# Scaled maxima of two attentions evicted by ScalarE and added by GpSimd, smaller VectorE chains, one context buffer, in a four-layer cross-attention stack

## What is computed

```python
# L0 (attentions 0 and 1): queries, keys and values without bias, 16 heads of 16
energy = einsum('bhsk,bhtk->bhst', Q, K)
lengths = sum(energy[:, :, 0, :] != 0, axis=-1)          # per head, from row 0
energy = where(cols >= lengths, -inf, energy)            # causal mask too in attention 0
z = softmax(energy / sqrt(dk)) @ V * mask                # mask: tokens with any feature != 0
x = layernorm(x + z)                                     # then relu feed-forward behind attention 1
# L1 (2 and 3): biases, output weights, masks given; gelu feed-forward (1024) behind attention 3
# L2 (4): 16 heads of 64, no mask.   L3 (5): 16 heads of 16, biases
```

## Time and profile before

| | |
|---|---|
| median of 3 runs | 2408.44 us (2404.12 to 2409.41) |
| the profiled execution | 2405.55 us, its span 2403.8 us |
| busy: TensorE, VectorE, ScalarE, GpSimd | 2345.7, 1541.7, 1368.9, 856.5 us |
| first TensorE instruction | at 4.04 us, after ScalarE's copies of the identity |
| first products of K and Q | 8.30 to 12.08 us |
| first scores | at 17.49 us |
| slot of attention 0 in the first round | 8.60 us from scores step to scores step |

### The profile page before, as it was taken

How to read it: one execution, slowest core, us unless ns; L and a number is a source line. 1 busy time by engine, 2 the same in 40 slices (tenths; PEclk the granted TensorE clock), 3 DMA queues, 4 the chain that set the end, 5 groups by cost and what they waited for, 6 DMA issues and landing times.

```text
span 2403.8 us, 73575 instructions
## 1 busy us (share of the span) xinstructions
PE 2345.7 (98%) x30353; PEld 1975.7 (82%) x30353; DVE 1541.7 (64%) x3410; ACT 1368.9 (57%) x3238; POOL 856.5 (36%) x1444
## 2 busy tenths in 40 slices
PE   8999999999989999999998999999999899999998
PEld 6788888888778888888877888888887788888887
DVE  6886654446888664444688866444478886644446
ACT  4556655546556666554655666654465566655455
POOL 2464322223346432222334743222333463312232
PEclk9999999999999999999999999999999999999999
DMA  5300000000100000000010000000001000000000
GB/s 157 133 3 2 3 2 1 1 1 11 44 5 2 3 2 2 1 1 1 17 40 2 2 3 2 1 1 1 1 24 33 2 2 3 2 2 1 1 1 19
DMA packets 23789, 32.48 MB, mean 14 GB/s; under 512 B 2304, under 2 KB 22176, under 8 KB 23328
## 3 DMA queue, kind: packets, MB, share of 16 engines
q1 hardware_dynamic: 23456, 27.78, 3.6%
HBM read 23.57 MB, written 4.19 MB: 12 GB/s over the span
## 4 chain that ended last, share of the span: by engine, by line
PE 90%; POOL 3%; DVE 3%; issue 3%; ACT 1%; DMA 0%; SPq 0%; POOLq 0%; DVEq 0%; ACTq 0%
PE M L580 51%; PE SC L776 14%; PE M L586 10%; PE M L810 6%; PE SC L792 3%; PE M L827 3%; PE SC L624 2%; POOL Kx L1344 1%; DVE nmax L1223 1%; POOL seen_diag L1361 1%; POOL Y L1370 1%; POOL rstd L1376 0%; ACT Pr L973 0%; POOL q L1331 0%; ACT Qx L952 0%
## 5 line engine op out<-in xcount | busy, mean ns | idle before, releaser
L580 PE MATMUL M<-XT,W 128*128 128x128 f32 x4096 | 523.3, 277 | 0.0
L580 PEld LDWEIGHTS M<-XT,W 128*128 128x128 f32 x4096 | 490.6, 192 | 13.7 <-issue 3.3
L1223 DVE TENSOR_REDUCE nmax<-SC 128x8 f32<-128x1024 f32 x320 | 390.5, 1220 | 121.0 <-PE SC L776 120.2
L1344 POOL TENSOR_SCALAR Kx<-K,own,k_ones 128x128 f32<-128x128 f32 x640 | 289.0, 466 | 313.5 <-PE SC L776 225.6
L776 PE MATMUL SC<-Kx,Qx 32*128 32x128 f32 x5120 | 365.6, 280 | 14.9 <-DVE Kx L1202 8.8
L776 PEld LDWEIGHTS SC<-Kx,Qx 32*128 32x128 f32 x5120 | 317.4, 186 | 71.4 <-issue 59.9
L982 ACT ACTIVATE Pr<-SC 128x1024 f32<-128x1024 f32 x256 | 263.2, 1028 | 191.2 <-PE SC L776 191.2
L776 PE MATMUL SC<-Qx,Kx 32*128 32x128 f32 x5120 | 371.6, 283 | 0.1
L1376 POOL TENSOR_TENSOR rstd<-rstd,half 128x1 f32<-128x1 f32 x256 | 171.7, 671 | 502.4 <-DVE rstd L1297 500.5
L776 PEld LDWEIGHTS SC<-Qx,Kx 32*128 32x128 f32 x5120 | 310.4, 186 | 2.9 <-issue 2.4
L952 ACT ACTIVATE Qx<-M,q_bias,q_scale 128x128 f32<-128x128 f32 x640 | 241.1, 460 | 122.5 <-PE M L580 120.9
(11 more groups left out here) (144 smaller groups left out, 4091.4 us busy)
## 6 DMA issues: line engine op xcount, KB each, us to landing
X<-x SPq DMA_DIRECT2D x32, 128.0 KB, 2.2
c_in<-ctx_in SPq DMA_DIRECT2D x32, 128.0 KB, 2.2
out<-X SPq DMA_DIRECT2D x32, 128.0 KB, 1.7
RV<-row_vec SPq DMA_DIRECT2D x1, 2304.0 KB, 8.7
W<-w_k SPq DMA_DIRECT2D x5, 256.0 KB, 4.0
W<-w_q SPq DMA_DIRECT2D x5, 256.0 KB, 4.1
W<-w_v SPq DMA_DIRECT2D x5, 256.0 KB, 3.9
W<-w_f SPq DMA_DIRECT2D x1, 1024.0 KB, 6.4
```

Source lines behind the costliest of these rows:

```text
L580: last = pe.matmul(dst, a, b, start=(k == 0), stop=(k == len(lhsTs) - 1))
L1223: dve.tensor_reduce(nm, SC[h][:, :].rearrange("p (g c t) -> p g c t", c=KC, t=P), AX_X, ALU.max, negate=True).then_inc(maxima, 1)
L1344: last = pool.tensor_scalar(kx[:, half_of, c * P:(c + 1) * P], k[:, c * P:(c + 1) * P], own[:, half_of:half_of + 1], k_ones[:, half_of, c: ...
```

## The change

Nine things change.

1. In attentions 0 and 1, ScalarE evicts the transposed maxima with the scale `spare` into a new `max_row` (one buffer), and GpSimd adds both halves to `Qx` in one instruction (*max rows*). The step ST waits for that addition (`rows_added`).
2. The length chain: the count comes out of the comparison (`accum_out`), so the reduction goes; `steps` holds whole numbers and the factor is in `spare_big`.
3. The comparisons with 0 of seen tokens go from VectorE to GpSimd.
4. The addition of eps goes from VectorE to GpSimd (*rstd* now two instructions); `mv` has two buffers.
5. One context buffer: the load of sequence b waits until TensorE has turned b-1.
6. VectorE's setup: memsets first, masks last, and a semaphore `scales_done` ahead of the masks, for which ScalarE's Q and GpSimd wait.
7. TensorE makes the mask tables as its fourth step, behind the first K and Q.
8. SyncE doesn't wait for the setup, except for the mask rows.
9. The tables NARROW, OWN and BROAD have new numbers for nearly all items.

```diff
-NARROW = dict(XT=-1.22, SM=-1.27, K=-0.92, Q=-0.86, L=-0.4, V=0.3, CT=0.32, MT=0.86, PV=2.66, E1=3.2, E2=3.56,
+NARROW = dict(XT=-1.2, TM=-2.02, SM=-1.29, K=-0.92, Q=-0.86, L=-0.38, V=0.3, CT=0.15, MT=0.86, PV=2.62, E1=3.2,
...
-OWN = {0: dict(max=0.09, rXT=-0.07, V=0.44, q0=-0.67, residual=3.23, exp=0.06, rE1=0.09, keys=-1.37, rPV=0.23, K=-1.19,
-               rV=-0.04, MT=1.42, rK=-0.04, rMT=-0.16, rQ=-0.03, XT=-1.45, L=-0.44, PV=2.82, seen0=-1.26, Q=-0.58,
+OWN = {0: dict(max=0.11, rXT=0.04, V=0.46, q0=-0.8, residual=2.76, exp=0.07, rE1=0.11, keys=-1.31, rPV=-0.12, K=-1.1,
+               rV=0.04, MT=1.05, rK=0.09, rMT=0, rQ=-0.01, XT=-1.55, L=-0.4, PV=2.98, seen0=-0.63, Q=-0.58, CT=0.69,
+               LN=3.34, LNe=0.53, rL=0.01, seen1=4.35, E1=3.16, rCT=0.09, rMP=-0.29),
...
+MAX_BY_POOL = (0, 1)
...
-            put("POOL", n + o["SM"] - 0.20, "token mask", n)
+            put("POOL", n + o["TM"], "token mask", n)
...
-        tile(n + o["MT"], "DVE", o["rMT"], "MT", n)
+        if a in MAX_BY_POOL:
+            tile(n + o["MT"], "ACT", o["rMT"], "MT", n)
+            put("POOL", n + o["MT"] + o["rMP"], "max rows", n)
+        else:
+            tile(n + o["MT"], "DVE", o["rMT"], "MT", n)
...
-        put("SP", slot(b, 0) - 2.0, "context", b)
+        put("SP", slot(b, 0) - 0.75, "context", b)
...
-                    if b >= 2:
-                        sp.wait_ge(tile_full, done("tile", ("CT", b - 2)))
+                    if b >= 1:
+                        sp.wait_ge(tile_full, done("tile", ("CT", b - 1)))
...
-                if step == 1:
+                if step == 3:
                     make_tables()
...
-                        evicted(("MT", t_u // 2))
+                        if att(t_u // 2) in MAX_BY_POOL:
+                            pe.wait_ge(rows_added, done("max_rows", t_u // 2))
+                        else:
+                            evicted(("MT", t_u // 2))
...
+                elif kind == "MT":
+                    n = it[1]
+                    i = AT["max_rows"][n]
+                    if i >= 1:
+                        act.wait_ge(rows_added, i)
+                    for half_of in range(2):
+                        last = act.activation(max_row[0][:, half_of, :], tile_of(it)[:, 0:P], ACT.Copy,
+                                              scale=spare[:, half_of:half_of + 1])
+                    last.then_inc(tile_act, 1)
...
-                    dve.tensor_scalar(ne[:, :], tile_of(it)[:, 0:P], spare_row[:, 0:1], -1.0 / BIG, ALU.not_equal,
-                                      ALU.mult).then_inc(tile_dve, 1)
+                    dve.tensor_scalar(ne[:, :], tile_of(it)[:, 0:P], spare_row[:, 0:1], 0.0, ALU.not_equal,
+                                      ALU.add, accum_out=cnt[:, :]).then_inc(tile_dve, 1)
                     dve.wait_ge(tile_dve, done("tile_dve", it))
-                    dve.tensor_reduce(cnt[:, :], ne[:, :], AX_X, ALU.add).then_inc(len_cnt, 1)
-                    dve.wait_ge(len_cnt, done("length", n))
...
+                elif kind == "max rows":
+                    n = it[1]
+                    pool.wait_ge(tile_act, done("tile_act", ("MT", n)))
+                    q = on_ring(Qx, "narrow", n)[:, :, :].rearrange("p h (c t) -> p h c t", t=P)
+                    pool.tensor_tensor(q, q, on_ring(max_row, "max_rows", n)[:, :, :].unsqueeze(2)
+                                       .to_broadcast([P, 2, KC, P]), ALU.add).then_inc(rows_added, 1)
...
                 elif kind == "rstd":
                     key = it[1:]
+                    pool.wait_ge(var_done, done("norm", key))
...
+                    pool.tensor_scalar(r[:, :], on_ring(mv, "norm", key)[:, 1:2], EPS, None,
+                                       ALU.add).then_inc(eps_done, 1)
                     pool.wait_ge(eps_done, done("norm", key))
```

More of the change, by code:

```diff
@@ L230, in make_orders @@
             put("DVE", n + o["seen1"], "seen1", b)
+            put("POOL", n + o["seen1"] + 0.02, "seen1", b)
         if a in XT_FOR_FF:
@@ L304 @@
     "q0": [it[1] for it in pick("POOL", {"q0"})],
+    "max_rows": [it[1] for it in pick("POOL", {"max rows"})],
     "e1": [it[1] for it in pick("DVE", {"E1"})],
@@ L420, in build @@
         x_loaded, stored = [sem(f"x_loaded{i}") for i in range(LANES)], [sem(f"stored{i}") for i in range(LANES)]
-        c_loaded, m_loaded = [sem(f"c_loaded{i}") for i in range(2)], sem("m_loaded")
-        ready_act, ready_dve = sem("ready_act"), sem("ready_dve")
+        c_loaded, m_loaded = sem("c_loaded"), sem("m_loaded")
+        ready_act, ready_dve, scales_done = sem("ready_act"), sem("ready_dve"), sem("scales_done")
         setup = sem("setup")
@@ L690, in _ @@
                     b = it[1]
[L691 to L692 removed]
+                    pe.wait_ge(c_loaded, 16 * (b + 1))
+                    turn(tile_of(it), c_in[0], KC).then_inc(tile_full, 1)
                 elif kind == "BT":
@@ L1028, in then @@
                 dve.wait_ge(setup, n)
+            dve.memset(half[:, :], -0.5)
+            dve.memset(ones_b[:, :], 1.0)
+            for i in range(3):
+                dve.memset(V16[i][:, :, DK:DK + 1], 1.0)
+                dve.memset(V16[i][:, :, DK + 1:32], 0.0)
+            dve.memset(mask_i[:, :], 0)
+            for i in range(2):
+                dve.memset(nmax[i][:, :], 0.0)
+                dve.memset(q0[i][:, :, :], 0.0)
             dve.wait_ge(consts_in, 16)
@@ L1068, in _ @@
             at = CB_AT["q4"]
-            dve.tensor_scalar(CB[:, at:at + 8], CB[:, at:at + 8], DK2 ** -0.5, None, ALU.mult)
-            for i in range(3):
-                dve.memset(V16[i][:, :, DK:DK + 1], 1.0)
-                dve.memset(V16[i][:, :, DK + 1:32], 0.0)
-            dve.memset(mask_i[:, :], 0)
-            for i in range(2):
-                dve.memset(nmax[i][:, :], 0.0)
-                dve.memset(q0[i][:, :, :], 0.0)
+            dve.tensor_scalar(CB[:, at:at + 8], CB[:, at:at + 8], DK2 ** -0.5, None, ALU.mult).then_inc(scales_done, 1)
+            dve.wait_ge(all_masks_in, 16)
+            dve.tensor_scalar(Pr[2][0:BATCH, P:2 * P], Pr[2][0:BATCH, 0:P].bitcast(I32), 0.0, -BIG, ALU.is_equal,
+                              ALU.mult).then_inc(bias_done, 1)
+            dve.wait_ge(masks_in, 16)
+            dve.tensor_scalar(whole(0), Pr[1][:, 0:P].bitcast(I32), 0.0, -BIG, ALU.is_equal,
+                              ALU.mult).then_inc(mask_whole, 1)
             dve.wait_ge(masks_turned, 1)
@@ L1373, in _ @@
                     key = it[1:]
+                    pool.wait_ge(var_done, done("norm", key))
+                    i, r = AT["norm"][key], on_ring(rstd, "norm", key)
+                    if i >= 2:
+                        before = INDEX["norm"][i - 2]
+                        if scaled_by_act(before):
+                            pool.wait_ge(normed_act, done("norm_act", before))
+                        else:
+                            pool.wait_ge(normed, done("norm_end", before))
+                    pool.tensor_scalar(r[:, :], on_ring(mv, "norm", key)[:, 1:2], EPS, None,
+                                       ALU.add).then_inc(eps_done, 1)
                     pool.wait_ge(eps_done, done("norm", key))
-                    r = on_ring(rstd, "norm", key)
                     pool.tensor_tensor(r[:, :], r[:, :], half[:, :], ALU.pow).then_inc(rstd_done, 1)
```

108 lines of the change are left out of this document (53 added, 55 removed).

## The result

The changed kernel took 2412.54 us in the median of 11 runs (2411.73 to 2412.94), the kernel before 2407.01 on the same chip (2402.36 to 2410.33): 1.0022 times as long, with a 95% interval of 1.0014 to 1.003. It is slower by 0.2%. The forecast had 2425, slower by 0.8%: the sign and the named waits came, the size was three times too large. The profiled execution spans 2411.1 us against 2403.8, 7.3 more.

The account below looks back on a forecast made before the run. TensorE, busy 98% of the span, was taken as the bound; 25.2 - 3.0 - 3.8 - 1.8 - 1.0 + 6.8 + 0.2 - 4 = +18.6 us on 2405.55 gave 2424.2, stated as 2425, range 2385 to 2442.

Parts of the forecast that it names:

- The addition's lateness: Attention 0: GpSimd's addition, queued behind the residual, ends at T+4.00, so products start at T+4.10 instead of T+3.04.
- TensorE loses 1.05 us in each slot: Attention 0, 6 slots in 4 rounds with a residual ahead of the addition: 24 x 1.05 = +25.2 us (22 to 30).
- no change: stalls at half of mine: Rival: stalls of 24 x 0.5 us cancel the gains, 2405 to 2412 us; chance 0.10.
- The entry, -3.0: Attention 0's entry, rounds two to four: addition late by 1.05 + 1.2, old waits of 2.2 go; 3 x (1.2 - 2.2).
- Attention 1, +6.8: Attention 1 with feed-forwards: two length products a round wait for length rows behind GpSimd's queue, 8 x 0.85 us.
- Seen diagonal, -1.0: Attention 1: earlier mask removes 9.8 us of waits, only 1.0 us gained because another equally long cycle stands behind.
- Length chain, 0: VectorE's length count: a 286 ns reduction goes, an accumulator read-out comes; 0, at the far end 6 us of loss.
- Start, -4: First scores come sooner through reordered setup: 3 us for the first, 1 for the next; -4 us (-7 to 0).
- Maxima, -3.8: TensorE's waits for the maxima, 3.8 us over 4 rounds, go as VectorE loses some 1.4 us of work a slot.
- Rest, with the maxima -3.8 - 1.8 - 1.0 + 0.2 = -6.4: Smaller terms: maxima waits -3.8, key waits -1.8, seen diagonal -1.0, eps and seen operations on GpSimd +0.2 us.
- Context buffer and places in attentions 2 to 5, 0: One context buffer: 0, at worst 6 us in round one; shifted places in attentions 2 to 5: loss 0 to 8, taken as 0.
- The first rival: Addition ends by T+2.94 in attention 0, so its stalls go: 2388 us, or 2380 with diagonal waits given back; chance 0.30.

## Why the prediction was right or wrong

**The addition's lateness: right as a wait.** The forecast had 24 slots with a residual ahead of the addition, and in all 24 TensorE waits. In 16 of them it is for the addition itself: 0.98 to 1.20 us in the steady slots, by the mechanism named, and 2.12 at each later round's entry, where I had 1.05 + 1.2. The other eight (slot 7 and the first of attention 1) show 1.23 us for the length rows, which stand behind the same addition; I had not looked for what else queues there. The seventeenth wait of the table, 0.64 us in slot 2 of round one, has no residual ahead, only the keys.

**A wait is not a loss: the step that failed.** It is "TensorE loses 1.05 us in each slot", 24 x 1.05 = +25.2, which takes the whole wait for time. Against the kernel before, the steady slot is 0.88 us longer (9.49 against 8.61); against nearly the same order with VectorE adding, 0.57 (8.92). By that second measure slot 7 of the second round is 0.5 us longer for its 1.23 of wait, and the first slot of attention 1 is 0.4 shorter in spite of it. With VectorE adding, other things end late in these slots; what they are was not taken apart slot by slot. Priced by undoing it, the whole move costs 11.5 us (10.0 of it in attention 0), where my three terms 25.2 - 3.0 + 6.8 make 29.0. My rival "no change: stalls at half of mine", with a chance of 0.10, took 24 x 0.5 = 12 and so came to the measured time, for another reason than it gave: the stalls were there in full, and counted for less than half.

**The entry, -3.0.** By my terms slot 3 of a later round stays level (1.05 + 1.2 - 2.2). The old waits of 0.79 and 1.43 us went, as forecast, and that slot still grew by 1.2 us in rounds two and three, 0.3 in round four; but slot 2 ahead of it is 1.2 shorter, so that the two together are level, or 1 us shorter in round four. I had not looked at slot 2.

**Attention 1, +6.8: near as a sum, by luck.** The waits for the length rows rose from 9.2 to 16.5 us, by 7.3. But 8 us of that rise come from the eight waits of 1.23 us named above, while the old ones at the start and at the entry went down. Where I had put the term, in two length products a round beside the feed-forwards, the waits are 0.2 to 0.7 us each and 4 us in all. As time it is nil: attention 1 as a whole is level.

**Seen diagonal, -1.0.** The reason given, another cycle of the same length behind it, fits the traces: the second to fourth slots of attention 1 of a later round now show 0.95 us each of wait for the maxima, where 0.73, 0.73 and 0.18 for the diagonal stood. In the kernel before, taking the 9.8 us away by an earlier mask gained nothing and cost 6.2. But the value of the place depends on the order around it. With the new order a late mask costs 26.6 us, and with the addition on GpSimd as well 47.

**Length chain, 0.** I called it just in time and priced the accumulator at 0 to 286 ns. Its read-out takes 83 ns by the group shown, and undoing it costs 0.31 us a slot and 9.2 us in all. The zero was wrong: the chain is the second leg of attention 0's cycle, and its shortening paid for part of the addition's delay. By the Trainium skill, "VectorE: DVE Perf Modes", section "Two Vector instructions with no wait between them", an operation with accumulator output counts as two instructions; the trace agrees, it shows the 347 ns operation and the read-out as separate rows.

**Start, -4:** measured 5.1, within the bounds given; the first maxima come 3.2 us sooner and the next ones 1.9 more, where I had 3 and 1. **Maxima, -3.8:** the waits for them rose from 3.8 to 14.8 us instead of going. **Rest, with the maxima -3.8 - 1.8 - 1.0 + 0.2 = -6.4:** measured 0.9 in all, which is not told from nothing. **Context buffer and places in attentions 2 to 5, 0:** these attentions are level to 0.7 us a round.

Summed: forecast -4 + 29.0 - 6.4 = +18.6, measured -5.1 + 11.5 - 0.9 = +5.5. The first rival, the addition covered, did not come; with an addition 0.55 us shorter (half of it left out) the kernel took 2395. GpSimd's price for 512 columns, 1276 ns, lies 0.16 above the line drawn through the two rows; the 256-column addition that the halved run made took 727. It lies as far above the estimate of 1.12 us that is scaled from the figure of the Trainium skill, "GPSIMD Engine Reference", section "Performance versus the Vector engine".

**What stays open.** What ends nearly as late as the addition in each slot, so that a wait of 0.98 us is worth 0.57; why attention 0's entry is so sensitive to the keys' place (6 to 7 us a round), which was read from slot times and not tried further; and no run separates what in the new order makes a late mask cost 26.6 us with VectorE adding.

## What to carry to other kernels

Where steps follow each other in a cycle over several engines, add up the legs of the cycle between two steps of the bound engine; a wait shows only which leg ends last there, and work of the bound engine shifted between legs can move the wait without moving the time. A wait is not the price of what is waited for, and the way of removing it has a price too: here 30 us of waits behind the move were worth 11.5, and taking away 9.8 us of others by an earlier mask cost 6. When an operation is moved to a slower engine with an in-order queue, look also at what queues behind it: a third of the waits stood under another name.

## What the runs showed of the hardware

An accumulator's read-out is a row of its own on VectorE, 83 ns. On GpSimd an operation on one column is far from free: the epsilon's (L1415) took 403 ns on average (206 to 513), against the 728 ns of a 256-column addition:

```profile
L1415 POOL TENSOR_SCALAR rstd<-mv 128x1 f32<-128x1 f32 x256 | 103.1, 403 | 573.4 <-DVE mv L1312 573.4
```

The times of the changed kernel spread over 1.2 us in 11 runs, those of the kernel before over 8. This is not explained.
